# A two-layer decoder on one core: one wait of ScalarE moved, one PSUM copy given to VectorE, a row of bias matmuls taken one expert earlier, and the last output stored in two halves

## The reference

```
x = layernorm(x + rwkv_block(x))                 # scan over time, then a gated feed-forward
x = layernorm(x + memory_attention(x, ctx))      # softmax over 512 context + up to 256 own keys, a sigmoid gate
x = layernorm(x + mixture_top1(x))               # 8 experts of 512 hidden units, bias b1[expert], gelu, shared Wo
x = layernorm(x + sparse_attention(x))           # 16 heads, strided mask
x = layernorm(x + cross_attention(x, ctx))       # 16 heads of 64 over 512 context tokens
x = layernorm(x + mixture_top2(x))               # 8 experts, capacity 40, relu; the output
```

## Time and profile before

| what | value |
|---|---|
| runs of the kernel before | 1144.24, 1144.55, 1144.87 us, median 1144.55 |
| the profiled execution | 1142.77 us, its span 1140.7 us |
| busy | PE 1067.3 us (94%), DVE 723.4 (63%), ACT 645.7 (57%), POOL 166.9 (15%) |
| chain that ended last, by engine | PE 71%, DVE 10%, ACT 9%, issue 5% |
| granted TensorE clock | 0.998 of full speed |
| start of the memory attention's last copy | 69.57, 343.78, 617.85 and 892.50 us in the four groups |

### The profile page before, as it was taken

One profiled execution on the slowest core, in us unless ns is written; L12 is line 12 of the kernel. 1 busy time (PEld: TensorE's weight loads), 2 busy tenths in 40 slices (PEclk: granted clock), 3 DMA queues, 4 the chain that ended last, 5 costly groups with the idle time before them and its releaser, 6 DMA issues.

```text
span 1140.7 us, 23186 instructions
## 1 busy us (share of the span) xinstructions
PE 1067.3 (94%) x9137; PEld 674.1 (59%) x9137; DVE 723.4 (63%) x1837; ACT 645.7 (57%) x1432; POOL 166.9 (15%) x237
## 2 busy tenths in 40 slices
PE   8899999999999998999899999999999999999997
PEld 6563564556775456555686355555577636645566
DVE  6542676888653376788855248688875417678871
ACT  5560457775653165777566136677666505577724
POOL 3210400121020030021102022021212004000000
PEclk9999999999999999999999999999999999999999
DMA  8400000000000000000000000000000000000000
GB/s 253 128 1 1 1 2 11 1 20 1 1 11 1 1 1 2 10 20 2 2 2 10 0 1 2 11 2 20 2 1 10 1 1 1 2 1 2 1 2 10
DMA packets 21069, 15.76 MB, mean 14 GB/s; under 512 B 872, under 2 KB 18645, under 8 KB 20957
## 3 DMA queue, kind: packets, MB, share of 16 engines
q1 hardware_dynamic: 20932, 14.24, 4.2%
q10 hardware_dynamic: 24, 0.01, 0.0%
HBM read 13.18 MB, written 1.05 MB: 12 GB/s over the span
## 4 chain that ended last, share of the span: by engine, by line
PE 71%; DVE 10%; ACT 9%; issue 5%; DVEq 2%; SPq 1%; POOL 1%; POOLq 0%; DMA 0%; ACTq 0%
PE ps L769 10%; PE ps L1001 8%; PE ps L965 8%; PE ps L983 6%; PE ps L803 4%; PE ps L809 4%; PE ps L1010 3%; PE ps L1129 2%; PE ps L800 2%; PE ps L1138 2%; ACT arena L1440 2%; ACT arena L1203 2%; PE ps L903 2%; DVE nmax L2141 2%; PE ps L784 1%
## 5 line engine op out<-in xcount | busy, mean ns | idle before, releaser
L1203 ACT ACTIVATE arena<-ps 128x512 f32<-128x512 f32 (+6 forms) x300 | 162.7, 574 | 123.3 <-PE ps L983 56.8
L2141 DVE TENSOR_REDUCE nmax<-ps 128x1 f32<-128x512 f32 x256 | 164.0, 684 | 23.5 <-PE ps L965 22.9
L1440 ACT ACTIVATE arena<-ps,nmax 128x512 f32<-128x512 f32 x256 | 173.4, 684 | 8.1 <-DVE nmax L2141 4.8
L1612 POOL TENSOR_TENSOR rstd<-mv,neg_half 128x2 f32<-128x2 f32 x72 | 49.7, 692 | 706.2 <-DVE mv L1785 706.2
L2146 DVE COPY arena<-ps 128x512 f32<-128x512 f32 x128 | 88.2, 689 | 60.8 <-PE ps L983 60.8
L983 PEld LDWEIGHTS ps<-ident,arena 64*128 64x128 f32 x2048 | 76.4, 138 | 83.2 <-issue 42.6
L769 PE MATMUL ps<-big,w1a 128*128 128x512 f32 x256 | 118.4, 605 | 0.1
L983 PE MATMUL ps<-ident,arena 64*128 64x64 f32 x2048 | 92.2, 228 | 12.2 <-ACT arena L1203 6.2
L769 PEld LDWEIGHTS ps<-big,w1a 128*128 128x128 f32 x256 | 46.0, 189 | 55.9 <-issue 54.7
L2033 DVE TENSOR_TENSOR big<-XT,ps 128x512 f32<-128x512 f32 x32 | 22.0, 687 | 89.9 <-PE ps L754 89.6
L1366 ACT ACTIVATE big<-ps 128x512 f32<-128x512 f32 x16 | 9.6, 597 | 117.6 <-PE ps L769 117.6
(11 more groups left out here) (389 smaller groups left out, 1998.5 us busy)
## 6 DMA issues: line engine op xcount, KB each, us to landing
ctx<-in_ctx_dram SPq DMA_DIRECT2D x4, 512.0 KB, 4.2
w1a<-in_L_ffn_W_dram SPq DMA_DIRECT2D x1, 2048.0 KB, 9.4
w1b<-in_L_ffn_W_dram SPq DMA_DIRECT2D x1, 2048.0 KB, 11.7
w2b<-in_L_ffn_W_dram SPq DMA_DIRECT2D x8, 256.0 KB, 5.8
X<-in_x_dram SPq DMA_DIRECT2D x4, 256.0 KB, 2.9
out_dram<-Y SPq DMA_DIRECT2D x4, 256.0 KB, 2.3
arena<-in_L_xattn_Wq_dram SPq DMA_DIRECT2D x1, 512.0 KB
arena<-in_L_xattn_Wk_dram SPq DMA_DIRECT2D x1, 512.0 KB
```

The costliest lines, as they stand in the source:

```text
L1203: return act.activation(dst, src, ACT.Copy)
L1440: act.activation(cprob[:, 2 * (t % 2) + h, :], bank(2 * (t % 2) + h), ACT.Exp, bias=nmax[:, s:s + 1], accum_out=rsum[:, j % 2, s:s + 1]).t ...
L2141: dve.tensor_reduce(nmax[:, s:s + 1], bank(s % 4), AX.X, ALU.max, negate=True)\
```

## The change

Four edits. ScalarE's wait for `cols_ready` 6 goes from the end of its start-up to the head of `sparse_attention`, where the scaled biases are first read. The copy of tile 3's turned probabilities goes from ScalarE to VectorE, into `gated(0)`, with a semaphore of its own (`pT_last`). The bias matmuls stand behind experts 2, 3, 4 and 5 and not behind 3, 4, 5 and 6. In the last group VectorE takes add and moments of half 0 before it waits for half 1, and SyncE stores each half when it is normalised.

```diff
@@ SyncE
-            store(ITERS - 1)
-            sp.wait_ge(out_stored, 16 * ITERS + 1)
+            for seq in range(GROUP):
+                r = slice(seq * QT, (seq + 1) * QT)
+                sp.wait_ge(out_ready, (ITERS - 1) * GROUP + seq + 1)
+                sp.dma_start(at(out_v, ITERS - 1)[:, r, :], Y[:, r, :]).then_inc(out_stored, 16)
+            sp.wait_ge(out_stored, 16 * (ITERS + 1) + 1)
@@ TensorE, values(t) of the memory attention
-                    pe.wait_ge(pT_ready, it * TT + t + 1)
+                    if t < TT - 1:
+                        pe.wait_ge(pT_ready, it * (TT - 1) + t + 1)
+                    else:
+                        pe.wait_ge(pT_last, it + 1)
@@ TensorE, experts of mixture_top1
-                    h = e - (E - 1 - HT)
+                    h = e - 2
                     if 0 <= h < HT:
                         if h == 0:
                             pe.wait_ge(b1_placed, 32)
@@ ScalarE, first_recurrent
-                act.wait_ge(cols_ready, 6)
@@ ScalarE, memory
-                for t in range(TT):
+                for t in range(TT - 1):
                     n = CTX + (t % QT + 1) * P
                     act.wait_ge(pT_ps, it * TT + t + 1)
-                    lo = 0 if t == TT - 1 else 4 * 512
-                    copy(probT[:, t // (TT - 1), 0:n], psf[:, lo:lo + n]).then_inc(pT_ready, 1)
+                    copy(probT[:, 0, 0:n], psf[:, 4 * 512:4 * 512 + n]).then_inc(pT_ready, 1)
@@ ScalarE, sparse_attention
+                act.wait_ge(cols_ready, 6)
@@ VectorE, gated(seq) of the memory attention
+                    if seq == 0:
+                        n = CTX + QT * P
+                        dve.wait_ge(pT_ps, it * TT + TT)
+                        dve.tensor_copy(probT[:, 1, 0:n], psf[:, 0:n]).then_inc(pT_last, 1)
                     dve.drain()
                     dve.wait_ge(alpha_ready, it + 1)
@@ VectorE, mixture_top2 of the last group
                     combined()
-                    for seq in range(GROUP):
-                        add_mixture(seq)
...
-                    layer_norm(it, 6, added, Y, Y, out_ready)
+                    layer_norm(it, 6, add_mixture, Y, Y, out_ready)
```

More of the change, by code:

```diff
@@ L339, in decoder_kernel @@
         pT_ps, pT_ready, av_ps = semaphore("pT_ps"), semaphore("pT_ready"), semaphore("av_ps")
+        pT_last = semaphore("pT_last")
         route_ps, onehot_ready = semaphore("route_ps"), semaphore("onehot_ready")
@@ L2283, in add_mixture @@
                     dve.drain()
-                def added(seq):
-                    pass
                 if more:
```

## The result

The changed kernel takes 1135.37 us, the median of four runs (1136.29, 1133.84, 1136.28, 1134.46), against 1144.57 for the kernel before on the same chip (1144.24 to 1144.87, four runs). The ratio is 0.9918, its interval 0.9904 to 0.9931: faster by 9.2 us in the medians, where 7.5 had been summed. The profiled execution is the one of 1136.29 us, with a span of 1134.1. Its span is 6.6 us shorter than that of before (1140.7).

A forecast was written before the change was run, and what follows sets the result against it. TensorE, busy 94% of the span, was taken to bound the kernel, so gains come from its idle places and gaps. 1.90 + 3.44 + 1.1 + 1.1 = 7.5 us off 1144.55 gave 1137.0 us, range 1135.0 to 1139.6.

The forecast's parts named there:

- case (a): All four gains arrive as summed, within 1.5 us: 1135.5 to 1138.5 us; chance 0.68.
- case (b): Layer norm does not hold TensorE back, so moving the copy gives its whole wait: 8.9 us, 1135.7; chance 0.10.
- edit 2: Memory attention, tile 3's copy moved to VectorE: 0.95 us in three groups, 0.59 in the second, sum 3.44 us.
- the last line of the sum: Gain subtracted from the median of before, 1.8 us above its profiled execution: 1144.55 − 7.5 = 1137.0 us.
- Edit 1: Start-up, ScalarE's wait for the scaled biases moved later: TensorE takes the whole shift, worth 1.90 us, once.
- About 0.14 of it stays: Start-up: of 0.17 us from the wait's release to the Exp table load, about 0.14 remains as entry of the group loop.
- The cover of 0.6 us: Memory attention: VectorE's moved copy ends 0.6 us before the gate it waits for, so it costs VectorE nothing.
- The chain of late things: Memory attention: half 1's layer norm moves by 0.54 us only and is late next; TensorE waits 0.3 us for it.
- The front of the edit: Memory attention: with the copy on VectorE, TensorE starts tile 3's values 1.20 to 1.26 us earlier.
- Edit 3: Experts, bias matmuls one expert earlier: a fourth pair costs 0.22, a lone one saves 0.50; 0.28 us a group, 1.1 in all.
- Edit 4: Tail of the last group: half 0's moments earlier give 0.70 us, the split store 0.4; sum 1.1 us.
- Rival (e): Slower: TensorE's clock falls to 1.2 GHz, beginning at the memory attention's new wait for X of half 1; 1146.9 us, chance 0.02.

## Why the prediction was right

The time lies in the range, 0.4 us above its lower end, and 1.6 us under the 1137.0. It is 0.1 us below the span that I gave to case (a), 1135.5 to 1138.5, and nearer to the 1135.7 of case (b); by its mechanism it is (a), whose four terms all came in, while (b), the whole wait of edit 2, did not happen. Of the 1.6 us, 0.5 are the terms and the rest is the last line of the sum. Step by step:

- **Edit 1, 1.90.** Measured 2.02. "About 0.14 of it stays" for the entry of the loop was wrong: the table load follows the copy that ScalarE is still doing at once, so the entry is probably hidden behind it. TensorE took the whole shift, and nothing in front of it became late, as argued.
- **Edit 2, 3.44.** Measured 3.62. The copy's price, 0.96, taken from the reduction of the same shape, is what the row shows. The Trainium skill, VectorE: DVE Perf Modes (section on the TRN2 errata), gives an estimate of 0.93; the trace has 0.96, and it was hidden by either. The cover of 0.6 us was 0.64. The chain of late things came out as written, the norm of half 1 as what ends last and TensorE's wait of 0.30 for it; the term in it that was too small is the 0.54 by which that norm moves, measured 0.65. So the first and third group gave 1.03 for 0.95, and the second 0.67 for 0.59. The front of the edit is 1.31 us and not 1.20 to 1.26, but that only makes the wait longer. The fourth gave 0.89 and not 0.95: it gets 1.01 up to the routing matmuls (L746) like the first, and loses 0.12 behind them, where the trace has VectorE's 0.42 us without work at 897.24. I had counted on such a stretch in the second group alone. Rival (b), the whole wait, is refuted by the longer row of transposes and by stretch (2): 3.62 and not 4 × 1.20 = 4.8.
- **Edit 3, 1.1.** Measured 1.20, 0.30 a group for 0.28. The second bf16 matmul of a pair costs 0.22, a lone one 0.50 to 0.51, and the gap between experts 6 and 7 closes to nothing.
- **Edit 4, 1.1.** Measured 1.19: 0.70 by the moments of half 0 under TensorE's matmuls, and 0.49 by the store (2.3 us for 256 KB, 1.8 for 128), where I took 0.4. The Trainium skill, DMA: Bandwidth & Descriptors (rules for kernel authors), advises to coalesce many small transfers, and by the cost formula of the same page the half is an estimate of 0.3; the measurement is 0.5, and it decides. Splitting gained here all the same: only the end of the last piece counts at the end of this kernel, and the first piece flies beside the work.
- **The sum, 7.5 for 8.03,** all four terms slightly low. The second part of the 1.6 us, 9.2 − 8.03 = 1.2, is the last line of the sum: I subtracted from the median of before and took its 1.8 us above the profiled execution as a constant. The mean clocks of the runs suggest that it is in part TensorE's clock, and the profiled execution of before had no fall in its start-up. Nothing in the prediction provided for this 1.2 us beyond 0.5 for the scatter, so that the median still fell into the range is in part luck.
- **Rival (e).** Its mechanism exists, a fall to 1.2 GHz that costs 1.7 us in the changed kernel's profile, but at another place, ahead of anything that the change touches: in the start-up, between 20 and 30 us in the profiled executions of seven of the kernels here; most timed runs of before have a lower mean clock than its fastest, which fits it but doesn't show the place. At the new wait in the memory attention the clock is 1.00. I had judged it from one profile only, in which the start-up stood at 1.00.

## What to carry to other kernels

When work is moved to another engine to end a wait, follow the chain one consumer further and ask how much that engine can give: here 1.31 us came free in the first group and 0.31 were taken back by the next norm, and giving the same copy to ScalarE ahead of the gate, or putting a projection into the new wait, only changed which step came last. The stretches between two instructions of TensorE, the bounding engine, repeated to 0.02 us from kernel to kernel, and in this in-order pipeline without fixed times behind its start-up the four small steps added up; the scatter of the medians was larger than two of them. So measure such steps as stretches. Before a difference of medians is split up, compare the start-up and the granted clock of both profiles.

## What was not expected of the hardware

- The granted clock fell to 0.50 for 3.4 us while TensorE's rows show it busy 2.40 of 2.40 us and then 1.70 of 1.70; it fell during identity transposes behind four one-row matmuls, and whether it falls differs between executions of the same start-up. The Trainium skill, TensorE: Matmul & The Clock Gate (part 1), puts such a fall down to idleness, which these rows don't show; whether such work counts as busy for the clock was not tested here.
- One bf16 matmul of 512 columns between fp32 passes costs 0.50 us, a second one beside it 0.22.
- VectorE loses 0.42 to 0.43 us in the second group's memory attention to a stretch without work between two instructions, in both kernels; with the copy ahead of it, it fell one instruction earlier and was as long. It is not alone: the changed kernel's trace has eight such stretches of 0.42 to 0.48 us with nothing that VectorE waits for, and that of the kernel before nine of 0.39 to 0.48, at other instructions. What they are was not tested.
